# The second FFN product of four tile pairs by seven half products each, with weight sums made on GpSimd

## The chip, the cores and the metric

The kernel runs on one core of a Trainium2 chip. The metric is device time in microseconds (us) for one execution of the whole program. Its engines, by the names that the profile uses: PE (TensorE, matmuls), DVE (VectorE), ACT (ScalarE), POOL (GpSimd), SP (SyncE, which here issues the DMAs).

## The reference

A graph layer with weights scattered from an edge list, a routed mixture of experts, a second graph layer (aggregation over normalised edges), and at the end a quantised feed-forward block, the only part that the change touches. There are N = 1250 rows of D = 1024 features, and the hidden width is 4096.

```python
def _quant_weight(w):                       # values -s, 0, s
    s = jnp.clip(jnp.mean(jnp.abs(w)), EPS, None)
    wq = jnp.clip(jnp.round(w / s), -1.0, 1.0) * s
    ...
def _quant_act(x):                          # integers times one factor for a row
    scale = 127.0 / jnp.clip(jnp.max(jnp.abs(x), axis=-1, keepdims=True), EPS, None)
    xq = jnp.clip(jnp.round(x * scale), -128.0, 127.0) / scale
    ...
h = jax.nn.gelu(_bitlinear(x, w1), approximate=False)
return _bitlinear(h, w2)
...
x = x + _L1_ffn_ref(_layernorm(x, axis=-1)[None], L1_ffn_w1, L1_ffn_w2)[0]
```

## The kernel before

The rows are cut into NT = 10 tiles of 128. `x` holds all of them in SBUF. The engines are programmed separately and meet at semaphores; each engine works through its own list in order, so an instruction that waits holds up all that stands behind it.

The feed-forward stage begins when the aggregation of the second graph layer ends. Its weights lie in SBUF as ternary numbers in an 8-bit float, `w1q` and `w2q`; DVE rounded them (`weight_piece`), PE turned them in 64 pieces during the aggregation and ACT wrote them (L1646 for `w2q`; `s_fc` counts the pieces). For a tile `i` the stage does this:

- DVE, `quantise(i)` (L2350 to L2356): normalises the tile, takes the maximum, scales and rounds to `xq`. This needs `rstd` of the tile, which POOL computes (`rstd_tile`, L829). SP writes `xq` to DRAM (L737) and reads it back transposed into `xqt` (L742), all in `input_t(i)`.
- PE, `ffn_in(i)` (L1304): 8 groups of 8 matmuls of 128x512 into PSUM banks 0 to 3. ACT applies Gelu to each group (L1658) into `hf`.
- DVE, `quantise_hidden(i)`: a maximum of each group (L2365), a few operations on one column (L2368 to L2371), scaling (L2372), rounding to `hq` (L2378). SP writes `hq` to DRAM (L748, `hidden_rows`) and reads it back transposed into `hqt` (L755, `hidden_t`). For tile 0 and the last tile PE transposes instead (L1313) and ACT copies (L1651).
- PE, `ffn_out(i)` (L1333): 64 matmuls of 128x512, 32 contraction blocks times 2 column halves, into banks 4 and 5. DVE `result(i)` (L2384) adds the scaled product to `x` into `out_t`, and SP stores it (L767). The last tile has its own form, `last_out` on PE (L1345, L1348) and two column halves on DVE (L2414).

PE's order is `ffn_in(0)`, `ffn_in(1)`, `ffn_out(0)`, and then alternately `ffn_in(i + 1)` and `ffn_out(i)`. `ffn_in(0)` waits for `xqt` of tile 0 and, at its third group, for DVE to have read the last aggregated tile (`s_aggread`). `ffn_out(i)` waits for `hqt` of tile i and for `result(i - 1)`. DVE's order for each i is `quantise_hidden(i + 1)`, `quantise(i + 3)`, `result(i)`. POOL has nothing to do in this stage beyond the last two `rstd_tile`.

## Time and profile before

| what | us |
|---|---|
| median of 3 runs (1038.51 to 1039.71) | 1038.97 |
| the profiled execution, its own time | 1037.67 |
| its span in the trace | 1035.9 |
| PE busy | 973.9 (94%) |
| DVE busy | 706.9 (68%) |
| ACT busy | 433.7 (42%) |
| POOL busy | 127.7 (12%) |

The first three are wall times. A busy time is a sum over instructions and is not to be added across engines. What decides is who waits for whom in the last 285 us of the span, in which the feed-forward stage runs.

### The profile page before, as it was taken

How to read it: one execution, taken by the hardware profiler on the slowest of the kernel's cores; microseconds unless marked ns; L12 is line 12 of the kernel's file. 1: busy time of each engine (PE TensorE's matmuls, PEld its weight loads, DVE VectorE, ACT ScalarE, POOL GpSimd, SP SyncE). 2: the span in 40 equal slices, each digit the busy share in tenths (PEclk: the TensorE clock that was granted, in tenths of full speed). 3: DMA queues.
4: the chain of work that ended last, by engine and by line, in shares of the span. 5: the costliest groups of instructions: out<-in, count | busy, mean ns of one | idle time of the engine just before them, and what ended most of it. 6: DMA issues, size and time to landing. Idle time of an engine off the chain costs nothing.

```text
span 1035.9 us, 17352 instructions
## 1 busy us (share of the span) xinstructions
PE 973.9 (94%) x6781; PEld 536.5 (52%) x6781; DVE 706.9 (68%) x1038; ACT 433.7 (42%) x541; POOL 127.7 (12%) x139
## 2 busy tenths in 40 slices
PE   1799899997899999999979999999999999999998
PEld 0688655553556666555544444455544444444444
DVE  7999888787765566665779772777776555556441
ACT  5354436652455556564642120677543111222221
POOL 6300042230211100010043300010100000000000
PEclk9899899999799999999989999999999999999999
DMA  3800025664688989888555956799413554544431
GB/s 114 256 2 2 2 82 204 228 239 166 246 307 327 342 314 317 300 315 301 179 167 164 204 121 203 272 374 350 160 23 82 123 122 113 120 109 107 108 93 36
DMA packets 166144, 188.91 MB, mean 182 GB/s; under 512 B 126519, under 2 KB 126841, under 8 KB 161983
## 3 DMA queue, kind: packets, MB, share of 16 engines
q1 hardware_dynamic: 159679, 165.47, 49.9%
q0 software_dynamic: 6400, 22.55, 7.1%
q8 instruction: 44, 0.72, 0.3%
q14 instruction: 21, 0.17, 0.0%
HBM read 137.98 MB, written 35.33 MB: 167 GB/s over the span
## 4 chain that ended last, share of the span: by engine, by line
PE 84%; DVE 7%; DMA 3%; issue 3%; ACT 1%; SPq 0%; DVEq 0%; POOL 0%; ACTq 0%; POOLq 0%
PE ps L1108 20%; PE ps L1304 13%; PE ps L1333 12%; PE ps L1286 8%; PE ps L1231 8%; PE ps L1215 8%; DMA abs_e<-in_L_ffn_w 2%; PE ps L1172 2%; PE ps L1037 2%; PE ps L1072 1%; PE ps L964 1%; PE ps L991 1%; PE ps L982 1%; DVE o_key L1856 1%; DVE w1l L2113 1%
## 5 line engine op out<-in xcount | busy, mean ns | idle before, releaser
L1304 PE MATMUL ps<-w1q,xqt 128*128 128x512 fp8e4 x640 | 139.9, 379 | 0.6 <-issue 0.6
L1658 ACT ACTIVATE hf<-ps,fs 128x512 f32<-128x512 f32 x80 | 54.9, 687 | 183.2 <-PE ps L1304 183.2
L1333 PE MATMUL ps<-w2q,hqt 128*128 128x512 fp8e4 x576 | 126.4, 379 | 0.0
L2365 DVE TENSOR_REDUCE hm<-hf 128x1 f32<-128x512 f32 x80 | 54.2, 685 | 73.9 <-ACT hf L1658 73.9
L1304 PEld LDWEIGHTS ps<-w1q,xqt 128*128 128x128 f16 x640 | 62.5, 98 | 75.8 <-issue 1.0
L1333 PEld LDWEIGHTS ps<-w2q,hqt 128*128 128x128 f16 x576 | 56.1, 98 | 67.1
L1108 PE MATMUL ps<-wt_h,xt 128*128 128x512 f16 x320 | 85.3, 379 | 0.0
L1108 PE MATMUL ps<-gwt_h,xt 128*128 128x512 f16 x320 | 84.6, 379 | 0.2 <-issue 0.2
L1215 PE MATMUL ps<-xdh,w1h 128*128 128x314 f16 x256 | 76.3, 298 | 4.1 <-DVE w1l L2113 2.7
L1215 PE MATMUL ps<-xdh,w1l 128*128 128x314 f16 x256 | 75.7, 296 | 0.0
L1215 PE MATMUL ps<-xdl,w1h 128*128 128x314 f16 x256 | 75.6, 295 | 0.0
L829 POOL TENSOR_TENSOR rstd<-mv,consts 128x1 f32<-128x1 f32 (+1 forms) x40 | 29.1, 736 | 315.4 <-DVE mv L1782 229.2
L1286 PE MATMUL ps<-hs_h,at_h 128*128 128x512 f16 x200 | 59.5, 379 | 0.8 <-DVE hs_l L2331 0.8
L1286 PE MATMUL ps<-hs_l,at_h 128*128 128x512 f16 x200 | 59.5, 379 | 0.0
L1777 DVE BATCH_NORM_STATS2 stats<-x 128x6 f32<-128x512 f32 x76 | 48.8, 684 | 4.4 <-DVE rounds_i L1746 0.2
L1108 PEld LDWEIGHTS ps<-gwt_h,xt 128*128 128x128 f16 x320 | 30.3, 98 | 38.8 <-issue 4.5
L1231 PE MATMUL ps<-w2h,hth 128*128 128x512 f16 x128 | 48.6, 380 | 0.0
L1231 PE MATMUL ps<-w2h,htl 128*128 128x512 f16 x128 | 48.5, 379 | 0.0
L1231 PE MATMUL ps<-w2l,hth 128*128 128x512 f16 x128 | 48.5, 379 | 0.0
L1108 PE MATMUL ps<-gwt_l,xt 128*128 128x512 f16 x160 | 47.6, 379 | 0.0
L1108 PE MATMUL ps<-wt_l,xt 128*128 128x512 f16 x160 | 47.6, 379 | 0.0
L1108 PEld LDWEIGHTS ps<-wt_h,xt 128*128 128x128 f16 x320 | 30.1, 98 | 33.5 <-issue 0.4
(319 smaller groups left out, 1858.1 us busy)
## 6 DMA issues: line engine op xcount, KB each, us to landing
wstage<-in_L_ffn_w SPq DMA_DIRECT2D x32, 1024.0 KB, 11.0
abs_in<-in_L_ffn_w SPq DMA_DIRECT2D x18, 1024.0 KB, 6.7
abs_e<-in_L_ffn_w SPq DMA_DIRECT2D x14, 1024.0 KB, 5.5
fnat_b<-in_L_ffn_w SPq DMA_DIRECT2D x28, 512.0 KB, 7.7
fnat_a<-in_L_ffn_w SPq DMA_DIRECT2D x27, 512.0 KB, 6.0
eo_d<-eo SPq DMA_DIRECT2D x16, 512.0 KB, 3.0
hq_d<-hq SPq DMA_DIRECT2D x8, 1024.0 KB, 6.3
xs_d<-xs_all SPq DMA_DIRECT2D x10, 512.0 KB, 2.9
```

Source lines behind the costliest of these rows:

```text
L829: g.tensor_tensor(rstd[:, one], mv[:, one, 1], consts[:, 1:2], ALU.pow).then_inc(s_rstd, 1)
L1037: mm(ps[:, 0, :], id16[:, :], at_h[:, 0, 0:512], start=True, stop=True)
L1108: last = mm(ps[:, 2 * u + h, :], lhs[:, u, k, :], rhs[:, k, h * 512:(h + 1) * 512], start=(k == 0 and a == 0), stop=(k == KD - 1 and a == 2))
L1172: last = tr(bank16(b)[:, k * P:k * P + m], gx[0:m, s, c:c + P], id16[0:m, 0:m])
L1215: last = mm(ps[:, 6 + hb % 2, 0:CAP], lhs[:, k, hb * P:(hb + 1) * P], rhs[:, k, :], start=(k == 0 and a == 0), stop=(k == KD - 1 and a == 2))
L1231: last = mm(ps[0:m, (2 * s + h) % 3, :], lhs[:, k, s * P:s * P + m], rhs[:, k, h * 512:(h + 1) * 512], start=(k == 0 and a == 0), stop=(k ...
L1286: last = mm(ps[:, 2 * u + h, :], at_h[:, b, i * P:(i + 1) * P], rhs[:, b, h * 512:(h + 1) * 512], start=(b == 0 and a == 0), stop=(b == NT ...
L1304: last = mm(ps[:, n % 4, :], xqt[:, u, k, :], w1q[:, k // 2, n * 512:(n + 1) * 512, k % 2], start=(k == 0), stop=(k == KD - 1))
L1333: last = mm(ps[:, 4 + h, :], hqt[:, u, k, :], w2q[:, k // 2, h * 512:(h + 1) * 512, k % 2], start=(k == 0), stop=(k == KF - 1))
L1658: cp(hf[:, i % 2, n * 512:(n + 1) * 512], ps[:, n % 4, :], ACT.Gelu, scale=fs[:, i % 2, 3:4]).then_inc(s_ge, 1)
L1777: v.bn_stats(stats[:, h, :], x[:, i, h * 512:(h + 1) * 512]).then_inc(s_bn, 1)
L2365: last = v.tensor_reduce(hm[:, u, n:n + 1], hf[:, u, n * 512:(n + 1) * 512], AX.X, ALU.max, apply_absolute_value=True)
```

## The change

Tiles 1 to 8 are taken in four pairs (a, b) = (2p+1, 2p+2). In a pair, the left operand is a 2 by 2 arrangement of blocks (tile a or b; first or second half of the 4096 hidden features) and the weight is one as well (the same halves; first or second 512 columns). The second product of the pair is done by a Strassen scheme: seven products of 16 matmuls each (`M1` to `M7`, in the order `ORDER`), where `ffn_out` took eight such for two tiles. Tile 0 and tile 9 keep the plain product. The row scale can't be put into the sums, so the sums are made of integers (`hqt` in 16 bits, weights in 8 bits).

- **Weight sums on POOL:** `t3` = w22 - w12, `t2` = t3 + w11, `t4` = w21 - t2, then w12 in place becomes w12 - w11, and at the end `b12` gives the old w12 back for the last tile. Each sum is 16 instructions of 128x512. The first starts when `w2q` is complete (`s_fc`), ahead of the last two `rstd_tile`; M7 waits for `s_wsum` 1, M6 for 2, M5 for 4, the last product for 5.
- **Row sums on DVE:** four TENSOR_TENSOR of 128x2048 in 16 bits for a pair (L2523, L2529, L2531, L2534 of the new program). Ten pieces of 512 columns take the place of two `result` of 1024: ACT copies M1 to `shared`, two products are added to it (L2510), and parts are added to `x` with the row's factor (`hscale`).
- **Order:** PE does two `ffn_in`, then one pair. `quantise_hidden(1)` and `quantise(3)` stay ahead of `result(0)` on DVE, and PE waits for `result(0)` right behind `ffn_out(0)`. In a pair DVE rounds the hidden rows of tile c = 2p+3 between the sums and the evacuations.
- **Transfers:** hidden rows are stored and turned in two halves (L770, L782), each with a semaphore of its own, and on SP tile 2p+2's stand ahead of the input of tile 2p+4. Results are written in place in `x`, so `out_t` is gone. Some semaphores are merged: the load of `b1c` now counts in `s_wg`, for which the gate weights' first use waits (48 and not 32).

```diff
+            def weight_sum(out, a, b, op):
+                for c in range(KF // 4):
+                    for h in range(2):
+                        cols = slice(256 * h, 256 * h + 256)
+                        last = g.tensor_tensor(out[:, c, cols, :], a[:, c, cols, :], b[:, c, cols, :], op, saturate=False)
+                last.then_inc(s_wsum, 1)
+
+            with pool.Fori(0, NT - 2) as i:
                 rstd_tile(3 * NT + i, i)
+            pool.wait_ge(s_fc, 4 + 64)
+            weight_sum(t3, wq22, wq12, ALU.subtract)
+            for t in range(NT - 2, NT):
+                rstd_tile(3 * NT + t, t)
+            pool.wait_ge(s_agg, NT)
+            ...
+            weight_sum(t2, t3, wq11, ALU.add)
+            ...
+            weight_sum(t4, wq21, t2, ALU.subtract)
+            pool.wait_ge(s_f2, 1)
+            weight_sum(wq12, wq12, wq11, ALU.subtract)
+            pool.wait_ge(s_hq, 4 + 2 * (NT - 1))
+            pool.wait_ge(s_wsum, 4)
+            weight_sum(b12, wq12, wq11, ALU.add)
...
+            FACTORS = {1: (hqt[:, 1, 0:half, :], wq11, 4), 2: (hqt[:, 1, half:KF, :], wq21, 5), 7: (s3, t3, 6),
+                       6: (hqt[:, 1, 0:half, :], t2, 7), 5: (hqt[:, 0, 0:half, :], wq12, 4),
+                       4: (hqt[:, 0, half:KF, :], t4, 5), 3: (hqt[:, 1, half:KF, :], wq22, 6)}
...
+            def ffn_pair(p, end=False):
+                for m in ORDER:
+                    pair_waits(p, m)
+                    hold(pe)
+                    a, b, bank = FACTORS[m]
+                    for k in range(half):
+                        last = mm(ps[:, bank, :], a[:, k, :], b[:, k // 2, :, k % 2], start=(k == 0), stop=(k == half - 1))
+                    last.then_inc(s_pair, 1)
+                    if end and m in (5, 4):
+                        pe.wait_ge(s_hq, 4 + 2 * NT)
+                        hidden_t(0 if m == 5 else 1, 3)
...
-            ffn_out(0, 0, turned=0)
-            with pe.Fori(0, NT // 2 - 2) as j:
+            ffn_out(0)
+            pe.wait_ge(s_f2r, 1)
+            with pe.Fori(0, PAIRS - 1) as p:
                 for u in range(2):
-                    ffn_in(2 * j + 2 + u, u)
-                    ffn_out(2 * j + 1 + u, 1 - u)
...
+                    ffn_in(2 * p + 2 + u, u)
+                ffn_pair(p)
...
+            def pair(p):
+                a, b, c = 2 * p + 1, 2 * p + 2, 2 * p + 3
+                ...
+                hidden_maxima(c, 1)
+                dve.wait_ge(s_hqt, 32 * b - 16)
+                dve.wait_ge(s_pair, 7 * p)
+                v.tensor_tensor(s3[:, :, :], a1, b1, ALU.subtract).then_inc(s_rsum, 1)
+                ...
+                v.tensor_tensor(b1, b1, b2, ALU.add).then_inc(s_rsum, 1)
+                ...
+                v.tensor_tensor(a1, b1, a1, ALU.subtract).then_inc(s_rsum, 1)
+                ...
+                pair_part(p, 2, 5, a, 0, 2)
+                v.tensor_tensor(a2, a2, a1, ALU.subtract).then_inc(s_rsum, 1)
+                hidden_scaled(c, 1)
+                hidden_rounded(c, 1)
```

On POOL, at the end of its list, before: the last `rstd_tile` of the expert stage and the loop over the ten tiles.

```order
L829 TENSOR_TENSOR rstd<-mv,consts 128x1 x2
L915 UNCONDITIONAL_BRANCH
L915 ISA
L829 ISA
L829 TENSOR_TENSOR rstd<-mv,consts 128x1
L915 REGISTER_ALU
L915 COMPARE_AND_BRANCH
```

On POOL, the same place now; `t_189` is t3, `t_196` is t2, `t_197` is t4, `b_193` is b12, and `w2q<-w2q` is the sum in place.

```order
L961 TENSOR_TENSOR t_189<-w2q 128x512 x16
L870 TENSOR_TENSOR rstd<-mv,consts 128x1 x2
L961 TENSOR_TENSOR t_196<-t_189,w2q 128x512 x16
L961 TENSOR_TENSOR t_197<-w2q,t_196 128x512 x16
L961 TENSOR_TENSOR w2q<-w2q 128x512 x16
L961 TENSOR_TENSOR b_193<-w2q 128x512 x16
```

Behind the loop, which now covers eight tiles, stand 80 instructions of 128x512 on an engine that had none here.

On PE, the last tiles, before: from `ffn_in(9)` to the plain product of the last tile.

```order
L1304 MATMUL ps<-w1q,xqt 128x512 x64
L1333 MATMUL ps<-w2q,hqt 128x512 x32
L1313 MATMUL ps<-id_50,hq 128x128 x8
L1333 MATMUL ps<-w2q,hqt 128x512 x16
L1313 MATMUL ps<-id_50,hq 128x128 x8
L1333 MATMUL ps<-w2q,hqt 128x512 x16
L1345 MATMUL ps<-w2q,hqt 128x512 x8
```

On PE, the same place now: two `ffn_in`, the seven products of the last pair, and the last tile (`s_198` is the row sum s3).

```order
L1368 MATMUL ps<-w1q,xqt 128x512 x128
L1424 MATMUL ps<-w2q,hqt 128x512 x32
L1424 MATMUL ps<-t_189,s_198 128x512 x16
L1424 MATMUL ps<-t_196,hqt 128x512 x16
L1424 MATMUL ps<-w2q,hqt 128x512 x16
L1377 MATMUL ps<-id_50,hq 128x128 x8
L1424 MATMUL ps<-t_197,hqt 128x512 x16
L1377 MATMUL ps<-id_50,hq 128x128 x8
L1424 MATMUL ps<-w2q,hqt 128x512 x16
L1437 MATMUL ps<-w2q,hqt_end 128x512 x8
```

The first transposes of tile 9's hidden rows now stand behind five of seven products, and one group of 64 matmuls became one of 112 for two tiles.

On DVE, the last pair now, between the maxima of tile 9 and the evacuation of M6 (before, L2368 to L2378 followed the maxima directly).

```order
L2465 TENSOR_REDUCE hm<-hf 128x1 x8
L2523 TENSOR_TENSOR s_198<-hqt 128x2048
L2525 SCALAR_TENSOR_TENSOR x<-shared,hscale,x 128x512
L2529 TENSOR_TENSOR hqt<-hqt 128x2048
L2531 TENSOR_TENSOR hqt<-hqt 128x2048
L2503 SCALAR_TENSOR_TENSOR x<-ps,hscale,x 128x512
L2534 TENSOR_TENSOR hqt<-hqt 128x2048
L2471 TENSOR_REDUCE fs<-hm 128x1
L2472 TENSOR_SCALAR fs<-fs 128x1
L2473 TENSOR_TENSOR hscale<-fs,sw 128x1
L2474 RECIPROCAL fs<-fs 128x1
L2475 TENSOR_SCALAR hf<-hf,fs 128x4096
```

Six operations moved in ahead of the rounding of tile c, in each pair.

## Rows read from the trace of the kernel before

**Rows 1.** Chain of waits from 735 us: start, length, engine and line.

```profile
751.67 0.58 issue
752.25 24.33 PE ps L1304 x112
...
795.64 13.81 PE ps L1304 x64
```

**Rows 2.** Busy time of a stretch: length, PE, PEld, DVE, ACT, POOL, clock, DMA.

```profile
800.00:850.00 50.00, 50.00 (x233) 22.70 (x232) 29.37 (x42) 9.62 (x14) 0.00 (x0) 1.00 0.55 123
```

**Rows 3.** Timeline of DVE at the stage's start: start, length, operation, [idle before].

```profile
742.21 0.81 DVE L2350 TENSOR_SCALAR xn_f<-x,mv,rstd 128x1024 f32<-128x1024 f32 x1 [3.40 <-PE ps L1072]
...
753.29 1.28 DVE L2335 SCALAR_TENSOR_TENSOR x<-ps,dinv,x 128x1024 f32<-128x1024 f32 x1
...
788.85 2.29 DVE L2378 TENSOR_SCALAR hq<-hf 128x4096 f16<-128x4096 f32 x1 [3.43 <-PE ps L1313]
...
795.68 1.28 DVE L2384 SCALAR_TENSOR_TENSOR out_t<-ps,fs,x 128x1024 f32<-128x1024 f32 x1 [0.59 <-PE ps L1333]
```

**Rows 4.** Timeline of SP: the transposed load of tile 0's input.

```profile
748.88 1.16 SPq L742 DMA_TRANSPOSE xqt<-xq_d  x1
```

**Rows 5.** Timeline of ACT: the last pieces of the second weight.

```profile
736.78 6.46 ACT L1646 ACTIVATE w2q<-ps 128x1024 fp8e4<-128x1024 fp8e4 x6 [2.65 <-PE ps L1072]
```

**Rows 6.** Timeline of POOL: additions of 1024 columns, and an iota.

```profile
135.18 4.68 POOL L849 TENSOR_TENSOR x<-x,bias_b 128x1024 f32<-128x1024 f32 x2 [3.60 <-DVE xt L1958]
141.61 2.36 POOL L849 TENSOR_TENSOR x<-x,bias_b 128x1024 f32<-128x1024 f32 x1 [1.75 <-DVE xn L1933]
...
152.89 1.51 POOL L863 IOTA iota_lo<- 128x256 f16 x1
```

**Rows 7.** Timeline of DVE in the same places.

```profile
135.26 2.38 DVE L1759 TENSOR_TENSOR wgb<-wg,b0c 128x64 f32<-128x64 f32 x1
137.56 2.38 DVE L1762 SCALAR_TENSOR_TENSOR wgv<-wg,wgv 128x64 f16<-128x64 f32 x1
139.87 0.21 DVE L1764 TENSOR_TENSOR wgv<-v,wgv 128x64 f16<-128x64 f32 x1
...
153.15 1.81 DVE L1933 TENSOR_SCALAR xn<-x,mv,rstd 128x1024 f32<-128x1024 f32 x1
```

**Rows 8.** Timeline of POOL: the last two rstd.

```profile
749.63 0.92 POOL L829 TENSOR_TENSOR rstd<-mv,consts 128x1 f32 x1 [12.11 <-DVE mv L1782]
756.76 0.55 POOL L829 TENSOR_TENSOR rstd<-mv,consts 128x1 f32 x1 [6.20 <-DVE mv L1782]
```

**Rows 9.** Groups of DVE by shape: count, busy us, mean ns, idle before.

```profile
L2365 DVE TENSOR_REDUCE hm<-hf 128x1 f32<-128x512 f32 x80 | 54.2, 685 | 73.9 <-ACT hf L1658 73.9
...
L1850 DVE TENSOR_TENSOR o_src<-iota_j,tab 128x2048 f16<-128x2048 f16 x27 | 32.9, 1217 | 0.0
...
L2372 DVE TENSOR_SCALAR hf<-hf,fs 128x4096 f32<-128x4096 f32 x10 | 23.5, 2354 | 0.4
...
L2414 DVE SCALAR_TENSOR_TENSOR out_t<-ps,fs,x 128x512 f32<-128x512 f32 x2 | 1.5, 752 | 12.7 <-PE ps L1345 6.5 <-PE ps L1348 6.2
```

**Rows 10.** Timeline of PE: the first matmul behind a long idle.

```profile
257.98 0.29 PE L1143 MATMUL ps<-mask,tri 128*128 128x160 f16 x1 [6.81 <-DVE mask L2056]
```

**Rows 11.** Busy time and clock by stretch behind that idle, columns as in rows 2.

```profile
268.00:270.00 2.00, 2.00 (x6) 0.62 (x6) 0.97 (x6) 0.00 (x0) 1.58 (x2) 0.50 0.12 20
...
272.00:274.00 2.00, 2.00 (x7) 0.75 (x6) 2.00 (x1) 0.00 (x0) 0.00 (x0) 0.66 0.97 317
```

**Rows 12.** DMA issues from 740 us: KB each, median us to landing.

```profile
hq_d<-hq SPq DMA_DIRECT2D x8, 1024.0 KB, 6.3
...
xq_d<-xq SPq DMA_DIRECT2D x10, 256.0 KB, 3.5
...
xqt<-xq_d SPq DMA_TRANSPOSE x10, 3.1
hqt<-hq_d SPq DMA_TRANSPOSE x8, 6.4
```

More of the change, by code:

```diff
@@ L1342, in last_out @@
                     if 1 <= q <= 2:
-                        hidden_t(q + 1)
+                        hidden_t(q + 1, 3)
                     for k in range(8 * q, 8 * q + 8):
-                        last = mm(ps[:, 0, :], hqt[:, 1, k, :], w2q[:, k // 2, 0:512, k % 2], start=(k == 0), stop=(k == KF - 1))
+                        last = mm(ps[:, 0, :], hqt_end[:, k, :], w2q[:, k // 2, 0:512, k % 2], start=(k == 0), stop=(k == KF - 1))
                 last.then_inc(s_f2, 1)
+                pe.wait_ge(s_wsum, 5)
                 for k in range(KF):
-                    last = mm(ps[:, 1, :], hqt[:, 1, k, :], w2q[:, k // 2, 512:D, k % 2], start=(k == 0), stop=(k == KF - 1))
+                    cols = b12[:, k // 2, :, k % 2] if k < half else w2q[:, k // 2, 512:D, k % 2]
+                    last = mm(ps[:, 1, :], hqt_end[:, k, :], cols, start=(k == 0), stop=(k == KF - 1))
                 last.then_inc(s_f2, 1)
@@ L1355, in _ @@
             ffn_in(1, 1, first=True)
-            ffn_out(0, 0, turned=0)
-            with pe.Fori(0, NT // 2 - 2) as j:
+            ffn_out(0)
+            pe.wait_ge(s_f2r, 1)
+            with pe.Fori(0, PAIRS - 1) as p:
                 for u in range(2):
-                    ffn_in(2 * j + 2 + u, u)
-                    ffn_out(2 * j + 1 + u, 1 - u)
-            ffn_in(NT - 2, 0)
-            ffn_out(NT - 3, 1)
-            ffn_in(NT - 1, 1)
-            ffn_out(NT - 2, 0, ahead=True)
+                    ffn_in(2 * p + 2 + u, u)
+                ffn_pair(p)
+            for u in range(2):
+                ffn_in(NT - 2 + u, u)
+            ffn_pair(PAIRS - 1, end=True)
             last_out()
@@ L1650, in hidden_t @@
                 act.wait_ge(s_ht, 4 * last + q + 1)
-                cp(hqt[:, last, 8 * q:8 * q + 8, :].rearrange("p k c -> p (k c)"), bank16(7 - q % 2), ACT.Copy).then_inc(s_hc, 1)
+                rows, bank = (hqt_end, 3 - q % 2) if last else (hqt[:, 0, :, :], 7 - q % 2)
+                cp(rows[:, 8 * q:8 * q + 8, :].rearrange("p k c -> p (k c)"), bank16(bank), ACT.Copy).then_inc(s_hc, 1)
             def ffn_in(i):
-                act.wait_ge(s_hq, i + 1)
+                act.wait_ge(s_hq, 2 * i + 2)
                 for n in range(8):
@@ L1669, in _ @@
                     hidden_t(3, 0)
+                if i >= 3 and i % 2 == 1:
+                    p = (i - 3) // 2
+                    act.wait_ge(s_pair, 7 * p + 1)
+                    if p > 0:
+                        act.wait_ge(s_pairread, 1 + 10 * p)
+                    cp(shared[:, :], ps[:, 4, :], ACT.Copy).then_inc(s_first, 1)
             for q in range(4):
@@ L2387, in ffn, with pair_part @@
-            def ffn(i, u):
-                quantise_hidden(i + 1, 1 - u)
-                if not last_of(i, NT, 3):
-                    quantise(i + 3, 1 - u)
-                result(i, u)
+                v.scalar_tensor_tensor(out=x[:, i, :], in0=ps[:, 4:6, :].rearrange("p b c -> p (b c)"),
+                                       scalar=hscale[:, i:i + 1], in1=x[:, i, :], op0=ALU.mult, op1=ALU.add).then_inc(s_f2r, 1)
+            def pair_part(p, m, bank, t, h, n):
+                dve.wait_ge(s_pair, done(p, m))
+                cols = slice(512 * h, 512 * h + 512)
+                v.scalar_tensor_tensor(out=x[:, t, cols], in0=ps[:, bank, :], scalar=hscale[:, t:t + 1], in1=x[:, t, cols],
+                                       op0=ALU.mult, op1=ALU.add).then_inc(s_pairread, 1)
+                dve.wait_ge(s_pairread, 1 + 10 * p + n)
@@ L2407, in _ @@
             quantise(2, 0)
[L2408 to L2409 removed]
+            quantise_hidden(1, 1)
+            quantise(3, 1)
+            result(0, 0)
+            for p in range(PAIRS):
+                quantise_hidden(2 * p + 2, 0)
+                if 2 * p + 4 < NT:
+                    quantise(2 * p + 4, 0)
+                pair(p)
             for h in range(2):
                 cols = slice(h * 512, h * 512 + 512)
[L2412 to L2415 removed]
+                dve.wait_ge(s_f2, 2 + h)
+                v.scalar_tensor_tensor(out=x[:, NT - 1, cols], in0=ps[:, h, :], scalar=hscale[:, NT - 1:NT],
+                                       in1=x[:, NT - 1, cols], op0=ALU.mult, op1=ALU.add).then_inc(s_f2r, 1)
 _INS = ["x", "src", "dst", "edge_weight", "L0_gnn_bias", "L0_ffn_wg", "L0_ffn_w1", "L0_ffn_b1", "L0_ffn_w2", "L0_ffn_b2",
```

229 lines of the change are left out of this document (153 added, 76 removed).

## The prediction

> **What bounds the kernel now.** I read the chain of waits first, from the end of the aggregation on. From 752.25 us to the last result it consists of PE's instructions alone: groups of 64 matmuls of 13.81 us follow each other without a gap, so one matmul of 128x512 costs 13.81 / 64 = 0.2158 us at the full clock [rows 1]. The busy times say the same: in 50 us PE is busy for 50.00, DVE for 29.4, POOL for nothing [rows 2]. Two places at the start of the stage are tighter than that average. The chain has 0.58 us of nothing ahead of `ffn_in(0)` [rows 1]: the transposed load of its input is issued at 748.88 and such a load lands 3.1 us later, at 752.0 [rows 4, 12], so the path there is DVE's `quantise(0)` from 742.21 on. And DVE ends `result(0)` at 795.68 + 1.28 = 796.96, while PE goes on at 795.64 [rows 1, 3]. Before, nobody waited for that.
>
> **The change, part by part.**
>
> Matmuls: a pair took 128 and takes 7 x 16 = 112. Four pairs save 64 x 0.2158 = **13.8 us**, all on the path if nothing else becomes late.
>
> The wait for `result(0)`: PE now stands still until DVE has done it, behind `ffn_out(0)`. Even if DVE's time stays as it is, that is 796.96 - 795.64 = 1.3 us.
>
> The weight sums on POOL: the trace has no 8-bit addition on POOL. The nearest row is an addition of 1024 columns, two in 4.68 us or one in 2.36 [rows 6]; half the columns give **1.18 us** a piece. Bounds: 0.6 us, half of it, if narrow data went through at twice the rate; upwards the iota makes 256 columns in 1.51 us [rows 6], at which rate a piece would take 3.0. I take 1.18, since operation and engine are the same. POOL may start when ACT has written `w2q`, at 736.78 + 6.46 = 743.24 [rows 5]. The four sums for M5 are 64 x 1.18 = 75.5 us.
>
> What that does to DVE is the largest term. While POOL worked on its two additions, DVE's TENSOR_TENSOR of 64 columns took 2.38 us, and the next such one 2.38 again; a third, with POOL idle, took 0.21. They ended just as POOL's additions ended [rows 6, 7]. A TENSOR_SCALAR of 1024 columns took 1.81 us beside POOL's iota, and the same form 0.81 with POOL idle [rows 3, 6, 7]. The other way round, `rstd` took 0.92 us on POOL beside such an operation of DVE and 0.55 alone [rows 8]. So a DVE operation with two SBUF tensors, or a fast TENSOR_SCALAR between SBUF tensors, and a POOL instruction exclude each other, and in a row they take turns. The Trainium skill's "SBUF — State Buffer", section "SBUF: two separate sides", calls this an exclusive lock on a shared pair of ports, held for the whole instruction; by that rule, short pieces lower one wait, yet not the number of waits, and here the trace agrees.
>
> From 743.2 on, POOL always has a piece at work. DVE's operations of the excluded kinds up to `result(0)`: three left of `quantise(0)` (the product of columns L2353, L2355, L2356), four each in `quantise(1)`, `(2)`, `(3)`, one in each of the two statistics, and four each in `quantise_hidden(0)` and `(1)` with the rounding in halves: 3 + 12 + 2 + 8 = 25. Between two that follow each other POOL takes a whole piece, less the gap that DVE's 0.21 us operation slipped into, some 1.0 us; after a reduction it is about half, 0.6. With ten to sixteen of the first kind I estimate 25 x 0.81 = 20 us. DVE's idle time in this part of some 10 us (3.43 alone ahead of the rounding of tile 1 [rows 3]) takes up about 6 of them, the rest stays because Gelu sets the pace of tile 0's maxima. `result(0)` then ends at 796.96 + 20.4 - 5.6 = 811.8.
>
> PE gets there late too: `quantise(0)` with three waits makes `ffn_in(0)` 3.1 us late, and its third group waits for the last aggregated tile (L2335, 753.29 before [rows 3]), 2.4 us more after `quantise(1)`'s waits. These are part of the same delay: `ffn_in(2)` starts at 811.8 in place of 795.64, which costs **+16.2 us** in all (the 1.3 is in it). The idle stretch ahead of it is 11 us. After an idle of 6.81 us the granted clock was 0.50, with PE busy for the whole of 268 to 270 us, and it left that level only in 272 to 274 [rows 10, 11]: 0.50 is the 1.2 GHz level, and 5 us of dense work at it lose **+2.5 us**.
>
> First pair: `ffn_in(2)` and `(3)` end at 839.4, M1 and M2 at 846.3. POOL's four sums end at 743.2 + 75.5 + about 20 of DVE's operations in between = 839, and M5 stands at 855: no wait. DVE comes out of the contention with tile 3's maxima at 846.6, s3 takes 1.22 [rows 9], so M7 waits **+1.6 us**.
>
> Pairs 1 to 3, without POOL: at M7, 6.9 us after `ffn_in(c)`, DVE has done the last maximum (0.69 [rows 9], behind a Gelu that I take to be as long: 1.4 us) and s3 (1.2); at M6 two more sums and a part of 0.75, 7.0 in all against 10.4 [rows 9]. The second tile's rows are rounded some 6 us after its `ffn_in` (1.4, small steps, 2.35 and 2.3 [rows 3, 9]), M7 begins 13.8 + 6.9 = 20.7 after it and M6 at 24.2. A half store lies between the 3.5 us of 256 KB and the 6.3 of 1024, a half load between 3.1 and 6.4 [rows 12]; I take 4.4 and 4.2. The first half is there after 6 + 4.4 + 4.2 = 14.6, the second after 19, so both fit. I put these pairs at nothing; a gain beyond the matmuls is excluded, since PE alone sets their length. If a half load cost 6.4, the second would be there after 23.4 and each pair would lose 2 to 3 us by the sums that follow.
>
> Last pair: `b12` runs beside it. DVE has nine excluded operations from s3 to the rounding of tile 9: without POOL that rounding ends 14.4 us behind `ffn_in(9)` (six operations of 0.75 to 1.22 with a wait for M2, then 2.35 and 2.3), and PE asks at 5 x 3.45 = 17.3. Nine waits of about 0.8 make it 21.3: **+4.0 us**.
>
> The load of `b1c` in `s_wg`, the stores from `x`, and ACT's copy of M1 (0.7 us beside PE) I put at nothing: each has its wait elsewhere. With half the slack gone they still don't show.
>
> **Sum:** -13.8 + 16.2 + 2.5 + 1.6 + 4.0 = **+10.5 us**. Against the profiled execution 1037.67 + 10.5 = 1048.2; its time lies 1.3 below the median of the runs, so as a median 1038.97 + 10.5 = 1049.5, about 1049.
>
> What the "GPSIMD Engine Reference" of the Trainium skill (section "Elementwise — side-by-side cycle accounting") says would make it worse: some 2.6 cycles an element at 1.2 GHz for a 32-bit addition of two inputs. As an estimate from that page, 512 elements and its dispatch are 1.2 to 1.3 us a piece, and by the turns above the sum would be 5 us more.
>
> **Rivals.**
>
> *The sums are cheap (faster).* If an 8-bit piece takes 0.6 us, or DVE slips between pieces, each of the 25 turns costs 0.3 and fits into DVE's idle time: -13.8 + 1.3 + 0.8 to 2 = -11 us, 1028. The point from which it decides is a piece of about 0.95 us: there `result(0)` ends near 807, the last pair waits 1, and gain and loss cancel. For it: no row shows 8-bit work on POOL. Against it: the rate of the same operation in 32 bits, 1.18.
>
> *The sums are dear (slower still).* At 1.4 us a piece the turns cost 5 us more at the start and 5 at M7: +20, 1059. From 1.5 on, w12's sum ends after M5 wants it, and from there each 0.1 us costs 64 x 0.1 = 6.4 on PE itself; at 2.0, +65. For it: the iota's 5.9 ns a column.
>
> *The half loads are not halves.* If each lands as late as a whole one, 6.4 us, `hqt` is 3 us late in each pair: with the forecast's terms +22, 1061; without the contention -1.
>
> *The turns are right, but the saving isn't there:* seven products in single banks with other operands could run slower than 0.2158. `ffn_in` has the same form, one bank and eight matmuls in a row, and runs at 13.81 for 64 [rows 1]. I give it no weight.
>
> **How the numbers follow.** Forecast (pieces of 0.95 to 1.35 us, times 1040 to 1057): 0.50. Cheap sums (1026 to 1038): 0.33. Dear sums: 0.12. Late halves: 0.05. Of the forecast's 0.50, 0.02 falls below 1037 and 0.04 within 0.2% of the time before (2.1 us, about what a measurement of this kernel can tell from no change), and 0.01 of the cheap case is there as well: faster 0.34, same 0.05, slower 0.61. The range leaves out the cheapest end and the dearest: 1028 to 1062. For the forecast alone it is 1040 to 1057.
>
> **What would show it.** The POOL group of 128x512 gives the piece, and DVE's L2350 and L2372 of tiles 0 to 3, under their new numbers, its turns: 1 us above 0.81 and 2.35. PE's wait ahead of `ffn_in(2)` should be some 11 us, with a low clock behind it, and M7 of the first and the transpose behind M5 of the last pair should wait 2 and 4. Steady pairs should take 2 x 13.81 + 24.17 = 51.8 us. It is wrong if a piece is under 0.9 us, or if DVE's operations keep their length beside POOL.

## The result, and the profile of the changed kernel

The changed kernel took 1045.36 us as the median of 20 runs (1041.13 to 1050.02), the kernel before 1038.59 beside it (20 runs, 1035.51 to 1047.43). The ratio is 1.0059, with a 95% interval of 1.0043 to 1.0076: 0.6% slower. A ratio leaves out single slow runs, of which there is one below, the 1045.15 us of number 11. The profiled execution took 1045.36 us as well, with a span of 1043.6.

**Where PE stands still.** PE's waits from 735 us to the end, with total, number and longest:

```profile
PE ps L1377 <- DVE hq L2485: 7.8, 2, 6.2
PE ps L1368 <- DVE x L2496: 3.9, 1, 3.9
PE ps L1368 <- issue: 3.7, 2, 2.8
```

Before, the only one here was the 0.58 us of issue in [rows 1]. PE's timeline shows where they are (start, length, operation, wait ahead of it in brackets):

```profile
754.76 5.30 PE L1368 MATMUL ps<-w1q,xqt 128*128 128x512 fp8e4 x16 [2.76 <-issue]
761.02 20.88 PE L1368 MATMUL ps<-w1q,xqt 128*128 128x512 fp8e4 x96 [0.97 <-issue]
788.12 1.03 PE L1377 MATMUL ps<-id,hq 128*128 128x128 f16 x8 [6.21 <-DVE hq L2485]
...
813.66 29.45 PE L1368 MATMUL ps<-w1q,xqt 128*128 128x512 fp8e4 x128 [3.86 <-DVE x L2496]
...
1017.38 0.62 PE L1377 MATMUL ps<-id,hq 128*128 128x128 f16 x8 [1.61 <-DVE hq L2485]
```

The reader is to see three groups of waits. `ffn_in(0)` starts at 754.76 instead of 752.25 [rows 1]. The transposes of hidden tile 0 wait 6.21 us for its rounding. `ffn_in(2)` waits 3.86 for `result(0)` and starts at 813.66 instead of 795.64. The rest of the stage has one more wait, the 1.61 in the last pair.

**The clock behind each wait.** Stretches of the busy view, columns as in rows 2; the last but two is the granted clock:

```profile
756.00:758.00 2.00, 2.00 (x6) 0.76 (x5) 1.93 (x4) 0.38 (x1) 2.00 (x3) 0.50 0.00 0
...
790.00:792.00 2.00, 2.00 (x7) 0.65 (x5) 1.90 (x5) 0.21 (x1) 2.00 (x3) 0.50 0.00 0
...
814.00:818.00 4.00, 4.00 (x13) 1.53 (x12) 0.00 (x0) 0.69 (x1) 4.00 (x5) 0.62 0.33 74
818.00:822.00 4.00, 4.00 (x20) 1.77 (x19) 1.95 (x3) 1.37 (x2) 4.00 (x5) 1.00 0.69 131
```

The clock is at 0.50 (1.2 GHz) behind the first two waits and 0.62 on average in the 4 us behind the third. What it cost is in the lengths: 16 matmuls in 5.30 us, where the same row of number 6 below has 3.61 at full clock; transposes and two groups of 8 in 6.80 against 4.35 there; and 128 matmuls in 29.45, where the timeline of number 6 has 27.79.

**What POOL did.** Timeline of POOL: the four sums for the first pair, 16 pieces each, and two `rstd` (the fifth, for the last pair, took 23.33 us from 991.78):

```profile
743.64 19.16 POOL L961 TENSOR_TENSOR t<-w2q 128x512 fp8e4<-128x512 fp8e4 x16 [5.79 <-ACT w2q L1740]
762.75 1.07 POOL L870 TENSOR_TENSOR rstd<-mv,consts 128x1 f32<-128x1 f32 x2
763.79 16.88 POOL L961 TENSOR_TENSOR t<-t,w2q 128x512 fp8e4<-128x512 fp8e4 x16
780.75 24.31 POOL L961 TENSOR_TENSOR t<-w2q,t 128x512 fp8e4<-128x512 fp8e4 x16
809.88 17.82 POOL L961 TENSOR_TENSOR w2q<-w2q 128x512 fp8e4<-128x512 fp8e4 x16 [4.82 <-PE ps L1388]
```

One piece, from the view of that line (min, median, max in ns); this sum met no operation of DVE that could hold it up:

```profile
L961 POOL TENSOR_TENSOR t<-t,w2q x16: 1083/1086/1090, 763.8 to 779.6; 128x512 fp8e4<-128x512 fp8e4 x16
```

A piece is 1.09 us; sixteen without a gap start every 1.05 us, and the other sums are longer by DVE's turns.

**What it did to DVE.** Timeline of DVE; the last row is the operation of the 780.93 row again, now with POOL idle:

```profile
745.91 1.48 DVE L2456 TENSOR_SCALAR xn_f<-xn_f,fs 128x1024 f32<-128x1024 f32 x1
747.42 1.47 DVE L2457 TENSOR_SCALAR xq<-xn_f 128x1024 f16<-128x1024 f32 x1
...
773.41 7.29 DVE L2473 TENSOR_TENSOR hscale<-fs,sw 128x1 f32<-128x1 f32 x1
...
780.93 3.07 DVE L2475 TENSOR_SCALAR hf<-hf,fs 128x4096 f32<-128x4096 f32 x1
784.03 4.03 DVE L2485 TENSOR_SCALAR hq<-hf 128x2048 f16<-128x2048 f32 x2
...
831.55 2.35 DVE L2475 TENSOR_SCALAR hf<-hf,fs 128x4096 f32<-128x4096 f32 x1
```

The two operations of 1024 columns take 1.48 and 1.47 us, where the same two took 0.75 and 0.69 at 838.77 and 839.56, with POOL idle; that of 4096 takes 3.07 against 2.35. Each is 0.7 to 0.8 us more, one turn of POOL. The row to stop at is that of 773.41: a product of 128x1 elements that takes 0.16 us alone took 7.29. It ended at 780.70, where POOL's second sum ended (763.79 + 16.88 = 780.67). Seven pieces ran, one behind the other, while DVE waited. So the two engines did not take turns there. The 6.21 us wait of PE stands behind this one row. Beside number 1 below, the same program without POOL's sums, 20 operations of DVE are longer up to `result(0)`: this one by 7.1 us and 19 others by 14.1 together, 0.4 to 1.0 each. From 805.06 to 809.88 POOL stood idle, ahead of its fourth sum, and DVE's operations had their own length.

**Steady pairs.** Chain of waits, start and length:

```profile
843.11 24.17 PE ps L1424 x112
867.28 27.63 PE ps L1368 x128
894.91 24.17 PE ps L1424 x112
```

27.63 + 24.17 = 51.80 us a pair, without a gap.

**The difference in one sum.** Of the spans, 1043.6 is 7.7 more than the 1035.9 of before. The matmuls give -13.8. Waits up to `ffn_in(2)` give 2.18 (2.76 less the 0.58 of before) + 0.97 + 6.21 + 3.86 = 13.2. The low clock gives 1.7, 2.4 and 1.7 behind the three groups, together 5.8. The last pair gives 1.6. The stage starts 0.3 later (DVE's first row at 742.54, before at 742.21 [rows 3]). That is 7.1, with 0.6 left over. An estimate of it: 16 matmuls last 3.62 us to the end of the last one, and 3.45 to the start of what follows them without a gap, so each of the four new breaks costs 0.17.

### The profile page after: what moved, and what is told of

Its sections match the earlier page's. It is cut to its first block, busy times and chain, and to the rows that moved or that the text cites. A ratio compares the mean times of both kernels' runs of the same rounds, so it can differ in the third digit from the quotient of the medians.

```text
span 1043.6 us, 17451 instructions
## 1 busy us (share of the span) xinstructions
PE 964.4 (92%) x6717; PEld 531.2 (51%) x6717; DVE 770.7 (74%) x1096; ACT 436.9 (42%) x545; POOL 228.4 (22%) x219
## 4 chain that ended last, share of the span: by engine, by line
PE 76%; DVE 13%; DMA 4%; issue 4%; ACT 1%; POOL 1%; SPq 0%; DVEq 0%; ACTq 0%; POOLq 0%
PE ps L1172 20%; PE ps L1368 11%; PE ps L1350 8%; PE ps L1295 8%; PE ps L1424 8%; PE ps L1279 8%; DMA abs_e<-in_L_ffn_w 2%; PE ps L1236 2%; PE ps L1028 1%; PE ps L1136 1%; PE ps L1055 1%; DVE hq L2485 1%; PE ps L1046 1%; DVE hf L2475 1%; DVE w1l L2215 1%
## 5 line engine op out<-in xcount | busy, mean ns | idle before, releaser
L1368 PE MATMUL ps<-w1q,xqt 128*128 128x512 fp8e4 x640 | 144.5, 388 | 7.6 <-DVE x L2496 3.9
L2465 DVE TENSOR_REDUCE hm<-hf 128x1 f32<-128x512 f32 x80 | 51.8, 681 | 42.5 <-ACT hf L1753 42.3
L961 POOL TENSOR_TENSOR b<-w2q 128x512 fp8e4<-128x512 fp8e4 x16 | 23.3, 1494 | 164.1 <-DVE hq L2485 164.1
L925 POOL DMA_INDIRECT gx<-xs_d,tok_i x24 | 22.8, 948 | 162.8 <-PE ps L1236 149.1
L1424 PE MATMUL ps<-w2q,hqt 128*128 128x512 fp8e4 x256 | 57.2, 379 | 0.0
```

Source lines behind the costliest of these rows:

```text
L925: pool.indirect_dma_start(out=gx[0:m, n % 3, :], out_offset=None, in_=xs_d[:, :], in_offset=bass.IndirectOffsetOnAxis(ap=tok_i[0:m, n:n + ...
L961: last = g.tensor_tensor(out[:, c, cols, :], a[:, c, cols, :], b[:, c, cols, :], op, saturate=False)
L1368: last = mm(ps[:, n % 4, :], xqt[:, u, k, :], w1q[:, k // 2, n * 512:(n + 1) * 512, k % 2], start=(k == 0), stop=(k == KD - 1))
L1424: last = mm(ps[:, bank, :], a[:, k, :], b[:, k // 2, :, k % 2], start=(k == 0), stop=(k == half - 1))
L2465: last = v.tensor_reduce(hm[:, u, n:n + 1], hf[:, u, n * 512:(n + 1) * 512], AX.X, ALU.max, apply_absolute_value=True)
```

## The experiments

The later kernels follow from what the earlier ones showed. "The kernel before" was run beside each group and its median was 1037.2 to 1037.8 us. Diffs are against the changed kernel, except where another is named.

**1. Without the sums.** The products that read a sum read a quarter of the second weight instead, and nobody waits for a sum, so the output is not the reference's; the shapes and counts of PE's, DVE's and ACT's instructions are.

```
-            weight_sum(t3, wq22, wq12, ALU.subtract)
-            weight_sum(t2, t3, wq11, ALU.add)
...
-            FACTORS = {..., 7: (s3, t3, 6),
-                       6: (hqt[:, 1, 0:half, :], t2, 7), ..., 4: (hqt[:, 0, half:KF, :], t4, 5), ...}
+            FACTORS = {..., 7: (s3, wq22, 6),
+                       6: (hqt[:, 1, 0:half, :], wq21, 7), ..., 4: (hqt[:, 0, half:KF, :], wq22, 5), ...}
```

> The changed kernel without its five weight sums on POOL: each product takes a quarter of the second weight of the same shape in place of a sum, so tiles 1 to 8 and half of the last tile's product are not the reference's; PE, DVE, ACT and SP do the same work. Theory (POOL's pieces and DVE's operations exclude each other, and that is all that went wrong): the 64 matmuls saved come through, 13.8 us, less 1.3 us of waiting for result(0): 12 us below the kernel before, about 1027, with PE waiting only ahead of the second input product of the loop. Rival (the pair form itself, its row sums, halves and order, makes PE wait): it stays at 1040 to 1045.

Measured: 1027.06 us (1025.26 to 1028.50), ratio 0.9896 (0.9859 to 0.9932). All that PE waited for from 735 us on:

```profile
PE ps L1347 <- DVE x L2471: 1.8, 1, 1.8
PE ps L1347 <- issue: 0.9, 1, 0.9
```

The seven products save what was counted: 13.8 less the 1.8 us wait for `result(0)` and 0.3 more at the start is 11.7, and the span is 11.5 shorter than before (1024.4 against 1035.9; by the ratio 10.8). Everything else of the change (halves, the moved waits, the new sums of rows on DVE, the shared product) hides. The whole loss, from 0.9896 to 1.0059 or some 17 us, is the 80 pieces on POOL.

**2. The wait for `result(0)` moved.** PE waits for `s_f2r` at the first product of the pair, which is what first writes the banks that `result(0)` reads, and no longer ahead of `ffn_in(2)`.

```
@@ the pair's products
+                    pe.wait_ge(s_f2r, 1)
@@ ahead of ffn_in(2)
-            pe.wait_ge(s_f2r, 1)
```

> The changed kernel with PE's wait for result(0) moved from behind ffn_out(0) to the first product of the first pair, which is the first to write its banks. The profile of the changed kernel has 3.9 us of waiting there and a low clock behind it. Theory (DVE is only late, by its turns with POOL, and catches up within two tiles): those 3.9 us and some 1.8 us of low clock are won, some 4 to 5.7 us, 1040, within 0.3% of the kernel before. Rival (DVE is saturated up to the first pair, so that a wait taken away comes back at M7 or M6): under 1.5 us are won, 1044 or more.

Measured: 1039.74 us (1033.78 to 1042.17), ratio 1.0012 (0.9991 to 1.0033). PE's waits:

```profile
PE ps L1377 <- DVE hq L2485: 7.8, 2, 6.2
PE ps L1368 <- issue: 4.1, 2, 2.9
```

The third wait is gone with the low clock behind it, 5 us by the two ratios, and nothing took its place. The product of hidden tile 0 again took 7.27 us.

**3. The kernel before, with the sums added.** Eighty pieces of the same kind, at the same places of POOL's list, into four scratch slots that nobody reads; from the fifth on each piece waits on a semaphore that the piece four places before it raised.

```
@@ before.py
+                        if made[0] >= 4:
+                            pool.wait_ge(s_scr, made[0] - 3)
+                        g.tensor_tensor(scr[:, made[0] % 4, :, :], a[:, c, cols, :], b[:, c, cols, :], op,
+                                        saturate=False).then_inc(s_scr, 1)
```

> The kernel before, with the 80 additions of 128x512 in 8 bits on POOL at the places that the change gives them; their results go into four scratch slots that nobody reads, so the output is the reference's. Theory: turns with POOL cost DVE some 20 us up to result(0). PE's first input product starts 2 us late, the transposes of tile 0 wait some 6 us with a low clock behind them, and product 1 waits some 5 us for its rows: 10 to 18 us above the kernel before, 1049 to 1057. Rival (POOL's additions do not hurt; the changed order of DVE does): within 2 us of the kernel before.

Measured: 1065.75 us (1054.23 to 1068.67), ratio 1.0269 (1.0232 to 1.0306); the profiled execution is the one of 1054.23. Its waits of PE:

```profile
PE ps L1332 <- issue: 3.9, 2, 2.9
PE ps L1361 <- DMA hqt<-hq_d: 3.9, 1, 3.9
```

That POOL's additions leave DVE and PE alone is refuted: an unchanged computation becomes slower by them. The expectation was missed all the same: the median lies above the range, and the 6 us expected at the transposes of tile 0 are not there. The trace accounts for the profiled execution: 7.3 us of new waits, 3.1 of low clock (16 matmuls in 5.07 us, 64 in 15.66), and 5.9 by which the sums start later (749.11) than ACT was done with `w2q` before (743.24 [rows 5]), for a reason ahead of this stage. What took the other four runs to 1064 and more is in no profile and stays open, as do the 5.9 us. What it did show besides: no product of DVE took over 1.07 us here. Number 5 was made on the reading that these pieces had gaps. They had none: the last sum, which met no operation of DVE that could hold it up, took as long as the second of the changed kernel (16.88).

```profile
998.65 16.87 POOL L928 TENSOR_TENSOR scr<-w2q 128x512 fp8e4<-128x512 fp8e4 x16 [162.49 <-DVE hq L2406]
```

**4. Larger pieces.** Eight of 1024 elements a sum.

```
-                    for h in range(2):
-                        cols = slice(256 * h, 256 * h + 256)
-                        last = g.tensor_tensor(out[:, c, cols, :], a[:, c, cols, :], b[:, c, cols, :], op, saturate=False)
+                    last = g.tensor_tensor(out[:, c, :, :], a[:, c, :, :], b[:, c, :, :], op, saturate=False)
```

> The changed kernel with each sum in 8 pieces of 128x1024 in place of 16 of 128x512: the same elements, half as many turns, each 2.1 us and not 1.09. Theory of whole-instruction turns: DVE's operations up to result(0) wait about twice as long each, the sum of waits doubles, and the kernel comes out at 1055 to 1062. Rival (the two share the ports' bandwidth, so that only the amount of data counts): the time of the changed kernel, 1043 to 1046.

Measured: 1051.89 us (1050.50 to 1052.18), ratio 1.0129 (1.0095 to 1.0164). The pieces of the first sum (min, median, max in ns), and then, from DVE's timeline, one turn beside them:

```profile
L959 POOL TENSOR_TENSOR t<-w2q x8: 2000/2009/2457, 743.1 to 758.2; 128x1024 fp8e4<-128x1024 fp8e4 x8
```

```profile
745.28 2.39 DVE L2454 TENSOR_SCALAR xn_f<-xn_f,fs 128x1024 f32<-128x1024 f32 x1
```

An operation of 0.75 us takes 2.39 beside pieces of 2.00, and 1.48 beside pieces of 1.09: a turn costs the piece less some 0.35. Slower, as expected, yet less than the 1055 at which the expectation began. The turns did become dearer: up to `result(0)`, 18 operations of DVE were longer than in number 1 by 24.1 us together, 1.34 each, where the changed kernel has 0.74. But the product of hidden tile 0 took only 1.94 us, one piece, with no gap between the pieces.

**5. A gap between pieces.** Each piece waits for the one before on the semaphore `s_wsum`, which all 80 now raise; the other waits on it count accordingly.

```
-                        last = g.tensor_tensor(out[:, c, cols, :], a[:, c, cols, :], b[:, c, cols, :], op, saturate=False)
-                last.then_inc(s_wsum, 1)
+                        if turn[0] > 0:
+                            pool.wait_ge(s_wsum, turn[0])
+                        g.tensor_tensor(out[:, c, cols, :], a[:, c, cols, :], b[:, c, cols, :], op,
+                                        saturate=False).then_inc(s_wsum, 1)
```

> The changed kernel, with each piece of a sum on POOL waiting for the piece before it by a semaphore, as in the old kernel with scratch sums, where no operation of DVE waited for more than one piece. In the changed kernel one product of columns on DVE (tile 0's, 773 us) waited 7.3 us, over seven pieces of one sum that followed each other without a gap, and PE waited 6.2 us for what stood behind it, with a low clock after. Theory (back-to-back pieces can keep DVE out for several; a gap lets it in): that wait falls to about 1.1, PE's to under 1, and 5 to 8 us are won: 1038 to 1040. Rival (the long wait is due to what that sum reads, or to the moment at which DVE asks): 7 us stay, and the gaps make the kernel 0 to 3 us longer.

Measured: 1044.48 us (1040.78 to 1045.43), ratio 1.0066 (1.0043 to 1.0089). Missed. The pieces now start every 1.17 us instead of 1.05. The product of hidden tile 0 took 0.67 us instead of 7.29, as expected, but PE's timeline shows where the gain went:

```profile
807.75 29.83 PE L1370 MATMUL ps<-w1q,xqt 128*128 128x512 fp8e4 x128 [8.88 <-DVE x L2498]
```

PE reached `result(0)`'s wait earlier and stood there 8.88 us instead of 3.86. The expectation had left that wait out. DVE had been the later engine all along; the long product only decided at which of two places PE waited for it.

**6. Both: the gap and the moved wait.**

```
+                            pool.wait_ge(s_wsum, turn[0])
...
+                    pe.wait_ge(s_f2r, 1)
...
-            pe.wait_ge(s_f2r, 1)
```

> Pieces with a gap as above, and PE's wait for result(0) ahead of the first pair. Theory: the two savings add, 1033 to 1036, which would be faster than the kernel before. Rival (what is won comes back as a wait at M7, M6 or M5 of the first pair): 1038 or more.

Measured: 1035.85 us (1033.59 to 1038.34), ratio 0.9977 (0.9957 to 0.9996). As expected. PE's waits:

```profile
PE ps L1370 <- issue: 4.2, 2, 3.1
PE ps L1379 <- DVE hq L2487: 2.6, 1, 2.6
PE ps L1427 <- DVE s L2525: 2.4, 1, 2.4
```

The change is now 0.2% faster than the kernel before, at the edge of what the runs can tell. The gap alone was worth nothing that can be measured (1.0066 against 1.0059) and the moved wait alone 5 us; together they are worth some 8.5, since with both PE is held at neither place.

**7. The first sum later.** Number 6, with the first sum behind GpSimd's last two `rstd`.

```
@@ number 6
-            pool.wait_ge(s_fc, 4 + 64)
-            weight_sum(t3, wq22, wq12, ALU.subtract)
             for t in range(NT - 2, NT):
                 rstd_tile(3 * NT + t, t)
+            pool.wait_ge(s_fc, 4 + 64)
+            weight_sum(t3, wq22, wq12, ALU.subtract)
```

> As before this one, and the first sum stands behind the last two rstd, so it starts some 15 us later, when DVE has done the inputs of tiles 0 and 1 and the last aggregated tile. Theory (the late start of ffn_in(0), its third group and their low clock, 5 us together, come from turns in those 15 us): PE starts as in the kernel before, and 3 to 5 us more are won, 1029 to 1032; POOL then ends the fourth sum at some 843 us against M5's 842, so up to 3 of them can come back there. Rival (the turns only move to later operations that PE waits for just the same): no gain against the version with the early start.

Measured: 1046.78 us (1046.29 to 1049.06), ratio 1.0101 (1.0077 to 1.0124). Missed. The start is as in the kernel before (issue 0.56), but POOL's fourth sum and the product M5 that reads it meet:

```profile
826.04 27.65 POOL L965 TENSOR_TENSOR w2q<-w2q 128x512 fp8e4<-128x512 fp8e4 x16
...
854.02 6.32 PE L1427 MATMUL ps<-w2q,hqt 128*128 128x512 fp8e4 x16 [12.95 <-POOL w2q L965]
```

The four sums took 98 us from 755.7 instead of the 84 of the changed kernel (743.6 to 827.7), by the gaps and by more turns of DVE. M5 wanted the fourth at 841. POOL's own time is the second limit of this design.

**8. Smaller pieces.** Thirty-two of 256 elements a sum, in the changed kernel.

```
-                    for h in range(2):
-                        cols = slice(256 * h, 256 * h + 256)
+                    for h in range(4):
+                        cols = slice(128 * h, 128 * h + 128)
```

> The changed kernel with each sum in 32 pieces of 128x256. Theory: the wait of an operation of DVE in its turn is half as long, so about half of the loss up to result(0) is won; doubling the pieces cost 6.5 us, halving them should win 3 to 6, 1039 to 1042. If a piece has some 0.1 us of fixed cost, POOL's four sums take 6 us longer and end some 20 us ahead of M5 still. Rival (POOL takes more turns instead, so that the total stays): 1044 to 1046.

Measured: 1051.06 us (1044.53 to 1055.63, four runs; the profiled one is the slowest), ratio 1.0114 (1.0062 to 1.0165). Missed. DVE's timeline, and then PE's longest wait:

```profile
746.25 0.95 DVE L2456 TENSOR_SCALAR xn_f<-xn_f,fs 128x1024 f32<-128x1024 f32 x1
...
770.44 15.95 DVE L2473 TENSOR_TENSOR hscale<-fs,sw 128x1 f32<-128x1 f32 x1
```

```profile
PE ps L1377 <- DVE hq L2485: 13.5, 1, 13.5
```

The fair turns did get shorter (0.95 us against 1.48), but the product was kept out until the second sum ended at 786.4, through some 26 pieces of 0.64 us. It is the end of the sum that counts there, not the length of a piece. It happened a second time, in the last pair, with an operation that is not small: the row sum for M7, 1.22 us alone. DVE, then POOL's fifth sum, then PE's wait at M7:

```profile
1004.02 11.28 DVE L2523 TENSOR_TENSOR s<-hqt 128x2048 f16<-128x2048 f16 x1 [0.77 <-DMA hqt<-hq_d]
...
995.07 19.15 POOL L961 TENSOR_TENSOR b<-w2q 128x256 fp8e4<-128x256 fp8e4 x32 [159.57 <-DVE hq L2485]
```

```profile
PE ps L1424 <- issue: 6.7, 1, 6.7
```

The fifth sum ended at 995.07 + 19.15 = 1014.22, the row sum 1.1 us later at 1015.30, and M7 started at 1015.40. So the view puts 6.7 us to no releaser, and they are a second row of pieces that kept DVE out.

**9. The gap in the second sum alone,** with the moved wait.

```
@@ number 2
-            weight_sum(t2, t3, wq11, ALU.add)
+            weight_sum(t2, t3, wq11, ALU.add, first=1)
@@ in weight_sum
+                        if first is not None and 2 * c + h > 0:
+                            pool.wait_ge(s_wsum, first + 2 * c + h)
...
+                        if first is not None and 2 * c + h < 15:
+                            last.then_inc(s_wsum, 1)
```

> The changed kernel with s_f2r waited for late, at the pair's first product, and a semaphore wait between the 16 pieces of the second sum (t2) alone; the other four sums stay back to back. Theory (back-to-back pieces can keep VectorE's column product out until the sum ends, and here it is the second sum that did): the column product of hidden tile 0 that took 7.3 us takes under 1.1, PE's wait for hq(0) of 6.2 us falls to below 1, the other turns stay as they were, and the time is 1033 to 1037, the 1036 of the version with gaps in all sums or a little under it, since three sums are not made slower. Rival (the gaps in the other sums are what helped, for instance in the first sum, which shifts everything behind it): the long wait stays or moves to another sum, and the time is 1038 to 1041.

Measured: 1036.07 us (1033.67 to 1041.82), ratio 0.9992 (0.9972 to 1.0013). The product took 0.86 us and PE no longer waited for hq(0). It is number 6 over again: with the gap in the one sum, those in the others buy nothing that can be measured.

**10. The first sum behind both `rstd`, no gaps,** with the moved wait.

```
@@ number 2
-            pool.wait_ge(s_fc, 4 + 64)
-            weight_sum(t3, wq22, wq12, ALU.subtract)
             for t in range(NT - 2, NT):
                 rstd_tile(3 * NT + t, t)
+            pool.wait_ge(s_fc, 4 + 64)
+            weight_sum(t3, wq22, wq12, ALU.subtract)
```

> The changed kernel with s_f2r waited for late and the first sum put behind GpSimd's last two rstd operations (start about 755.7 instead of 743.6), all pieces back to back. Theory: ffn_in(0) starts as in the kernel before (750.8, issue wait 0.6), and the four sums end by about 755.7 + 19 + 17 + 24 + 18 = 834 plus small gaps, well before M5 at about 850, so the 13 us wait for the fourth sum, which the version with gaps had, is gone. What is open is the column product of hidden tile 0 (ready at about 766.4, now inside the first sum) and of tile 1 (786.8, inside the second): if a whole sum can keep it out whichever sum it is, one or both take 5 to 8 us and the time is 1036 to 1041; if only the second sum does that and tile 1 has slack, 1031 to 1036. Rival: the clock at the start of the stage or M7 takes what is won, over 1041.

Measured: 1040.49 us (1038.79 to 1042.24), ratio 1.0031 (1.0016 to 1.0046). DVE's product of tile 0, with the sum that it met, and PE's longest wait:

```profile
767.99 0.65 DVE L2473 TENSOR_TENSOR hscale<-fs,sw 128x1 f32<-128x1 f32 x1
...
756.99 21.36 POOL L961 TENSOR_TENSOR t<-w2q 128x512 fp8e4<-128x512 fp8e4 x16
...
849.33 6.25 PE L1425 MATMUL ps<-w2q,hqt 128*128 128x512 fp8e4 x16 [7.70 <-POOL w2q L961]
```

The time is in the range expected if a whole sum keeps the product out; the mechanism isn't. No product took over 1.07 us, although every sum ran back to back. The loss is M5's wait again, 7.7 us, where the expectation had the fourth sum end at 834 and it ended at 849. So pieces without gaps can keep DVE out, but need not. That weakens numbers 5 and 9 a little: here a shift in time alone, without a gap, left the product free as well, and the two pairs of kernels that differ by the gap (5 against the changed kernel, 9 against 2) have one trace a kernel.

**11. The first sum between the two `rstd`,** no gaps, with the moved wait.

```
@@ number 2
+            rstd_tile(3 * NT + NT - 2, NT - 2)
             pool.wait_ge(s_fc, 4 + 64)
             weight_sum(t3, wq22, wq12, ALU.subtract)
-            for t in range(NT - 2, NT):
-                rstd_tile(3 * NT + t, t)
+            rstd_tile(3 * NT + NT - 1, NT - 1)
```

> The changed kernel with s_f2r waited for late and the first sum put between GpSimd's last two rstd operations (start about 750) instead of before both (743) or behind both (757), all pieces back to back. Theory: the first quantisation runs beside an idle GpSimd, so ffn_in(0) starts at most 1.6 us later than in the version with the first sum behind both (752.2), and every sum ends some 6 us earlier than there, so PE's 7.7 us wait for the fourth sum at M5 and the low clock behind it (2.6 us) go for the most part: 1031 to 1036. Rival: the column product of hidden tile 0 is kept out of its port by a whole sum, as in the changed kernel; then PE waits up to 8 us for hq(0) and the time is 1037 to 1042.

Measured: 1032.17 us (1029.33 to 1045.15, 12 runs), ratio 0.9938 (0.9913 to 0.9962): 0.6% faster than the kernel before. POOL's first sum, and then PE's waits of over 0.2 us:

```profile
750.97 17.80 POOL L961 TENSOR_TENSOR t<-w2q 128x512 fp8e4<-128x512 fp8e4 x16
```

```profile
PE ps L1425 <- DVE s L2523: 2.0, 1, 2.0
PE ps L1368 <- issue: 1.8, 2, 1.2
PE ps L1377 <- DVE hq L2485: 1.5, 1, 1.5
PE ps L1425 <- DVE hqt L2531: 0.3, 1, 0.3
```

5.8 us of waits are left of the 15.4 of the changed kernel. The start at 751 lets `quantise(0)` run beside an idle POOL, and lets the fourth sum end at 838.4, ahead of M5 at 843. No product of DVE was kept out (0.45 and 1.07 us for tiles 0 and 1).

**12. The same with the gap in the second sum,** `weight_sum` as in number 9.

```
@@ number 11
-            weight_sum(t2, t3, wq11, ALU.add)
+            weight_sum(t2, t3, wq11, ALU.add, first=1)
```

> The same with a semaphore wait between the pieces of the second sum alone, which lengthens that sum by at most 3 us. Theory: within 2 us of the run without those waits if no column product was kept out there, and 1031 to 1036 if one was. Rival: M5 waits again for the fourth sum, by what the second got longer, 2 to 4 us more than without.

Measured: 1031.63 us (1029.32 to 1033.50), ratio 0.9937 (0.9915 to 0.9960). The same time as number 11, as expected where no product was kept out. Either is better than both kernels of this case.

## Why the prediction was right, and where its terms were off

The forecast was the contention case, +10.5 us in the profiled execution; measured +7.7 there, and 1045.4 against 1049 as a median. The mechanism held: POOL's pieces hold up DVE, DVE holds up PE at the start of the stage and in the last pair, and that outweighs 13.8 us of matmuls. Numbers 1 and 3 show it from both sides. That the sum came so close is in part luck: DVE's delay, its largest term, has the forecast's size with another make-up. Point by point:

- **Matmuls, -13.8.** Right: 24.17 us for 112, 51.80 a pair, and number 1 gave the rest back.
- **The piece, 1.18.** Measured 1.09, inside the bounds of 0.6 to 3.0 and above the point of 0.95 from which the cheap case would decide. The rival of cheap sums fell by that and by the turns (0.7 us each, not 0.3).
- **25 turns of 0.81, `ffn_in(2)` at 811.8.** It started at 813.66, or 17.7 later without the shift of 0.3, where 16.2 was forecast. The total was close, for a partly wrong reason: 13.2 of it are waits and 4.1 the low clock behind the first two, which the working did not have. On DVE, 25 turns and 20 us were forecast; measured are 19 turns of 0.74 us on average, 14.1 together, and one operation that cost 7.1, in sum 21.2. The step "in a row they take turns" failed at that one operation, which was kept out for seven pieces. The Trainium skill's "SBUF — State Buffer", section "SBUF: two separate sides", gives the pair of ports to whichever instruction starts first. That fits the turns of 0.7 us, and it says nothing on who is next when both wait, which the row of 7.29 us asks. The prediction had its turns from two additions of POOL beside two products [rows 6, 7], too few to show that a row of pieces can keep DVE out.
- **One long wait of 11 us ahead of `ffn_in(2)`.** Wrong in its place: it was 6.2 at the transposes of tile 0 and 3.9 at `ffn_in(2)`. Number 5 moved it from the one to the other with nothing gained, which shows that the sum and not the place is what DVE's delay fixes.
- **Low clock behind `ffn_in(2)`'s wait, +2.5.** Measured 1.7. The failing part is that the clock was low in two other places too, 1.7 and 2.4 us; the forecast had seen one idle stretch where there were three.
- **M7 of the first pair, +1.6.** Measured 0 in the changed kernel. POOL's fourth sum ended at 827.7 where the forecast had 839, so DVE had done s3 at 846.25; and PE came to M7 only at 849.85, where the forecast had 846.3. Its own terms leave nothing here either: the 2.5 us of low clock, which it adds to the sum, puts M7 at 848.8, behind its own s3 at 847.8. In numbers 6, 9, 10 and 11, where PE comes earlier, it is there with 1.5 to 2.4.
- **M5 of the first pair, 0.** Right in the changed kernel, by 29 us (827.7 against 857). Numbers 7 and 10 show that this cover can go: 12.9 and 7.7 us.
- **Last pair, +4.0.** Mis-sized: 1.6. Nine waits of 0.8 us were taken; seven operations of DVE were longer there, by 3.8 us in all.
- **Steady pairs, 0; late halves.** Right. The views of the DMA issues give a half store 5.1 us (taken 4.4) and a half load 4.7 (taken 4.2), with enough slack for both:

```profile
hq_d<-hq SPq DMA_DIRECT2D x16, 512.0 KB, 5.1
...
hqt<-hq_d SPq DMA_TRANSPOSE x16, 4.7
```

The sum was 2.8 us too high: +1.5 measured at the start of `ffn_in(2)`, -0.8 of clock behind it, -1.6 at M7, -2.4 in the last pair and +0.3 of shift are -3.0.

The prediction took the contention for granted once the sums were there. It did not ask where the sums start. That was worth more than the size of the pieces: with the same 80 pieces, number 11 is some 7.7 us faster than number 2, and 1.2% faster than the changed kernel, by their ratios.

## What to carry to other kernels

Work moved to GpSimd is free only if VectorE has slack in the same stretch. Count VectorE's operations with two SBUF tensors and its fast TENSOR_SCALARs there, at about one piece less 0.35 us each, and place the work so that the first VectorE chain that PE waits for runs ahead of it; 7 us of delay of the first sum, with one wait of PE put where its banks are really written, turned +0.6% into -0.6% here. Between pieces that must run beside VectorE's chain, a semaphore wait is a cheap insurance, at some 0.12 us a piece, against one operation being kept out for a whole row of them: it happened in three of the seven kernels here without such a gap and in none of the five with one. That the wait is what prevents it is likely and not proven. When a wait vanishes and the time stays, look whether the next wait for the same engine has grown by as much.
